# Graph attention kernel: value products joined two pairs at a time, softmax norms spread in two parts, last tile's messages pair by pair

## The reference, cut to what matters

```python
def _attention_message(Q, K, V, senders, receivers, n_nodes):
    scores = jnp.einsum('ehd,ehd->eh', Q[receivers], K[senders]) * scale
    smax = jax.ops.segment_max(scores, receivers, num_segments=n_nodes)
    ex = jnp.exp(scores - smax[receivers])
    denom = jax.ops.segment_sum(ex, receivers, num_segments=n_nodes)
    att = ex / denom[receivers]
    out = jax.ops.segment_sum(att[:, :, None] * V[senders], receivers, num_segments=n_nodes)
    return (out, att)
...
out = msg.reshape(n_nodes, HEADS * DV) @ W_ff.T + b_ff
```

## Time and profile before

| | |
|---|---|
| median of three runs | 321.08 us (320.94 to 321.26) |
| the profiled execution | 321.26 us, its span 319.5 us |
| TensorE busy, weight loads | 294.4 us (92% of the span), 226.4 us |
| VectorE, ScalarE, GpSimd busy | 194.0, 142.9, 69.8 us |
| chain that ended last | TensorE 81%, VectorE 12%, ScalarE 3%, issue 2% |
| TensorE's granted clock | full in all 40 slices |
| attention stage | from 219 us to the end |

### The profile page before, as it was taken

The page is one execution under the profiler, slowest core; times in us unless marked ns, Lnnn a source line. Parts: engine busy times, 40 slices in busy tenths (PEclk is TensorE's granted clock), DMA queues, the critical chain, the costliest instruction groups (busy, mean ns, idle before and its releaser), DMA issues.

```text
span 319.5 us, 5460 instructions
## 1 busy us (share of the span) xinstructions
PE 294.4 (92%) x2006; PEld 226.4 (71%) x2006; DVE 194.0 (61%) x471; ACT 142.9 (45%) x282; POOL 69.8 (22%) x97
## 2 busy tenths in 40 slices
PE   2848699999999999998999999997999999999994
PEld 1513345544677788687887889997888898888882
DVE  5899977986234344334359744967857565565721
ACT  1152234523325322533343505687876464665621
POOL 6045003210655044800012402310002020020202
PEclk9999999999999999999999999999999999999999
DMA  5753992111080300045300000000000000000000
GB/s 181 251 209 131 331 386 106 67 36 55 17 291 8 133 2 2 2 131 139 125 0 0 2 0 3 0 3 0 2 0 2 36 0 35 1 2 35 1 35 29
DMA packets 10970, 22.29 MB, mean 70 GB/s; under 512 B 950, under 2 KB 966, under 8 KB 10938
## 3 DMA queue, kind: packets, MB, share of 16 engines
q1 hardware_dynamic: 8772, 16.80, 15.3%
q0 software_dynamic: 800, 2.62, 2.2%
q10 hardware_dynamic: 1366, 2.45, 2.1%
HBM read 15.60 MB, written 6.26 MB: 68 GB/s over the span
## 4 chain that ended last, share of the span: by engine, by line
PE 81%; DVE 12%; ACT 3%; issue 2%; DMA 1%; DVEq 0%; POOL 0%
PE banks L1239 15%; PE banks L1185 9%; PE banks L1225 9%; PE banks L1325 8%; PE banks L1130 8%; PE banks L1311 7%; PE banks L1300 7%; PE banks L1083 5%; PE banks L1345 5%; DVE key_hot L820 3%; DVE row_hot L827 2%; PE banks L1215 2%; PE banks L1335 2%; PE banks L1172 1%; PE banks L1202 1%
## 5 line engine op out<-in xcount | busy, mean ns | idle before, releaser
L1003 DVE CUSTOM_DVE_ANT_0 s_sb<-banks,mask_add 128x640 f32<-128x640 f32 x40 | 32.6, 822 | 22.2 <-PE banks L1300 22.1
L1083 PE MATMUL banks<-key_hot,row_hot 128*128 128x480 f16 x120 | 32.5, 419 | 9.0 <-DVE key_hot L820 9.0
L660 ACT ACTIVATE p_sb<-s_sb,neg_max 128x640 f32<-128x640 f32 x40 | 32.9, 823 | 17.3 <-DVE neg_max L1003 17.3
L820 DVE TENSOR_SCALAR key_hot<-iota,picked 128x480 f16<-128x480 f16 x120 | 36.9, 374 | 0.0
L1185 PE MATMUL banks<-adjT,h 128*128 128x320 f16 x240 | 33.1, 299 | 0.4 <-DVE zT_even L879 0.4
L1083 PEld LDWEIGHTS banks<-key_hot,row_hot 128*128 128x128 f16 x120 | 12.6, 105 | 26.4 <-DVE key_hot L820 9.2
L1185 PEld LDWEIGHTS banks<-adjT,h 128*128 128x128 f16 x240 | 23.3, 98 | 9.8 <-DVE zT_even L879 0.7
L1311 PE MATMUL banks<-ident,p_sb 128*128 128x128 f32 x200 | 29.6, 275 | 0.2 <-ACT pT L667 0.2
L490 POOL TENSOR_TENSOR msgT<-msg_f,msgT 128x128 fp32r<-128x128 f32 x20 | 8.6, 458 | 95.7 <-ACT msgT L681 95.7
L1239 PE MATMUL banks<-w_hl,zT_even 128*128 128x512 f32 x120 | 29.2, 394 | 0.0
L1300 PE MATMUL banks<-k_hi,q_st 128*128 128x320 f32 x80 | 27.1, 348 | 2.0 <-DVE neg_max L1003 2.0
(11 more groups left out here) (176 smaller groups left out, 466.4 us busy)
## 6 DMA issues: line engine op xcount, KB each, us to landing
w_self<-in_L_gnn_W_self_dram SPq DMA_DIRECT2D x3, 1024.0 KB, 9.4
raw<-in_L_gnn_W_rel_dram SPq DMA_DIRECT2D x3, 1024.0 KB, 15.6
raw<-in_L_gnn_W_qkv_dram SPq DMA_DIRECT2D x3, 1024.0 KB, 5.3
sorted_rows<-zero_rows ACTq DMA_DIRECT2D x1, 1792.0 KB, 10.7
self_rows<-hs SPq DMA_DIRECT2D x7, 256.0 KB, 2.0
hs<-sorted_rows SPq DMA_DIRECT2D x1, 1280.0 KB, 7.2
xs<-in_x_dram SPq DMA_DIRECT2D x1, 1024.0 KB
raw<-in_L_gnn_W_ff_dram SPq DMA_DIRECT2D x1, 1024.0 KB
```

The lines of the kernel that those rows point to most:

```text
L660: nc.scalar.activation(p_sb[:, n % NPR, :], s_sb[:, n % NS, :], ACT.Exp, scale=-1.0, bias=neg_max[:, it, h:h + 1], accum_out=denom[:, it, ...
L820: return nc.vector.tensor_scalar(to_key, iota[:], float(KEYS * w), key, ALU.add, ALU.is_equal)
L1003: nc.vector.tensor_tensor_reduce(s_sb[:, n % NS, :].rearrange("p (a j) -> p a j", a=2), banks[:, c:c + 2, 0:HALF], mask_add[:, it, :].rear ...
L1083: mm(banks[:, w % 2, 0:KEYS], row_hot[:, w % 2, k, :], key_hot[:, w % 2, k, :], start=(k == 0), stop=True, skip_group_check=True).then_inc ...
```

## The change

Five parts:

1. **pv by twos.** The first pair of each two is placed at the second's place, so two pairs' products stand together, 40 instructions in the trace, at ten places instead of nineteen.
2. **norms in two parts.** VectorE spreads the eight norms to 128x512 itself (a broadcast copy into a float32r high part, then a subtraction for the low part), and rb becomes eight float32r products of 128 held columns with `ident_r` (128 columns) over all PSUM partitions. `norm` has one buffer instead of two, so norm n waits for rb n-1.
3. **`ident_r`**, a float32r copy of `ident`, is made on GpSimd at the start. `bounds` and `bounds_f` move to another place in SBUF.
4. **Banks of the last tile.** Its four pairs write banks 0 to 3 (the scores' banks, free after the last smax) instead of quarters of bank 4.
5. **Messages of the last tile.** Each waits for its own pair's pv alone.

```diff
-        placed += [(at, "pv", n) for n, at in enumerate(pv_at)]
+        placed += [(pv_at[n // 2 * 2 + 1], "pv", n) for n in range(NT * KD)]
...
+                pair_at = [max(pv_at[it * KD + a // 2 * 2 + 1], it * H + RB) + 0.1 for a in range(KD)]
+                placed += [(pair_at[a], "msg", it * KD + a) for a in range(KD)]
+                placed += [(pair_at[-1] + FF_STEP * kt, "ff", it * KD + kt) for kt in range(KD)]
+                placed.append((pair_at[-1] + FF_STEP * KD, "out", it))
...
+        def pv_place(it, a):
+
+            return banks[:, 4, a * P:(a + 1) * P] if it < NT - 1 else banks[:, a, 0:P]
...
+            nc.gpsimd.tensor_copy(ident_r[:], ident[:]).then_inc(s_ident, 1)
...
                 elif kind == "norm":
                     dve.wait_ge(s_exp, H * (n + 1))
-                    if n >= 2:
-                        dve.wait_ge(s_rb, n - 1)
+                    if n >= 1:
+                        dve.wait_ge(s_rb, n)
                     chain(nc.vector.reciprocal(recip[:, n % 2, :], denom[:, n, :]))
-                    nc.vector.scalar_tensor_tensor(out=norm[:, n % 2, :], in0=neg_max[:, n, :], scalar=BIG / 2,
-                                                   in1=recip[:, n % 2, :], op0=ALU.is_lt, op1=ALU.mult
-                                                   ).then_inc(s_norm, 1)
+                    chain(nc.vector.scalar_tensor_tensor(out=norm[:], in0=neg_max[:, n, :], scalar=BIG / 2,
+                                                         in1=recip[:, n % 2, :], op0=ALU.is_lt, op1=ALU.mult))
+                    spread = norm[:].unsqueeze(2).broadcast_to([P, H, DK])
+                    chain(nc.vector.tensor_copy(norm_hl[:, 0], spread))
+                    nc.vector.tensor_tensor(norm_hl[:, 1], spread, norm_hl[:, 0].bitcast(F32),
+                                            ALU.subtract).then_inc(s_norm, 1)
                 elif kind == "msg":
                     it, a = divmod(n, KD)
+                    if it == NT - 1:
+                        dve.wait_ge(s_pv, n + 1)
+                    elif a == 0:
+                        dve.wait_ge(s_pv, KD * (it + 1))
                     if a == 0:
-                        dve.wait_ge(s_pv, KD * (it + 1))
                         dve.wait_ge(s_rsb, it + 1)
...
-                    if a == 0 and it >= 1:
+                    if a == 0 and it == NT - 1:
+                        pe.wait_ge(s_smax, NT * H)
+                    elif a == 0 and it >= 1:
                         pe.wait_ge(s_msg, KD * it)
...
-                    for h in range(H):
-                        me = 64 * (h % 2)
-                        ins = mm(banks[me:me + 64, 7, h // 2 * P:(h // 2 + 1) * P],
-                                 norm[:, n % 2, h:h + 1].broadcast_to([P, DK]), ident[:],
-                                 start=(h < 2), stop=True, skip_group_check=True)
+                    for a in range(KD):
+                        for p in range(2):
+                            ins = mm(banks[:, 7, a * P:(a + 1) * P],
+                                     norm_hl[:, p, 2 * a:2 * a + 2, :].rearrange("p h d -> p (h d)"),
+                                     ident_r[:], start=(a == 0 and p == 0), stop=(p == 1), skip_group_check=True)
```

More of the change, by code:

```diff
@@ L81, in gnn_kernel @@
         ident = sb("ident", [P, P], F32)
+        ident_r = sb("ident_r", [P, P], F32R)
         ident16 = sb("ident16", [P, P], F16)
@@ L106, in gnn_kernel @@
         place_u = sb("place_u", [P, NT], U32)
-        bounds = sb("bounds", [1, 3, 32], I32)
-        bounds_f = sb("bounds_f", [1, 4, 32], F32)
         stats = sb("stats", [P, NT, 6], F32)
@@ L118, in gnn_kernel @@
         recip = sb("recip", [P, 2, H], F32)
-        norm = sb("norm", [P, 2, H], F32)
+        norm = sb("norm", [P, H], F32)
         Z_BYTES = 2 * KD * NP * 4
@@ L160, in gnn_kernel @@
         ones = place("ones", o_r4 + 60768, [P, P], F32)
+        bounds = place("bounds", o_r4 + 64000, [1, 3, 32], I32)
+        bounds_f = place("bounds_f", o_r4 + 64384, [1, 4, 32], F32)
         tile_iota = place("tile_iota", o_r4 + 61280, [P, 8], F32)
@@ L186, in gnn_kernel @@
         self_d = nc.dram_tensor("self_rows", [SP, D], F32, kind="Internal").ap()
+        norm_hl = place("norm_hl", o_r4 + 35328, [P, 2, H, DK], F32R)
         banks = ctx.enter_context(nc.psum_tensor("banks", [P, 8, 512], F32))
         s_fill = sem("s_fill")
+        s_ident = sem("s_ident")
         s_edges = sem("s_edges")
@@ L325, in gnn_kernel @@
             placed += [((it + 1) * H, "norm", it), (it * H + RB, "rb", it)]
-            placed += [(msg_at, "msg", it * KD + a) for a in range(KD)]
-            placed += [(msg_at + FF + FF_STEP * kt, "ff", it * KD + kt) for kt in range(KD)]
-            placed.append((msg_at + FF + FF_STEP * (KD - 1) + 0.1, "out", it))
+            if it < NT - 1:
+                placed += [(msg_at, "msg", it * KD + a) for a in range(KD)]
+                placed += [(msg_at + FF + FF_STEP * kt, "ff", it * KD + kt) for kt in range(KD)]
+                placed.append((msg_at + FF + FF_STEP * (KD - 1) + 0.1, "out", it))
+            else:
+                pair_at = [max(pv_at[it * KD + a // 2 * 2 + 1], it * H + RB) + 0.1 for a in range(KD)]
+                placed += [(pair_at[a], "msg", it * KD + a) for a in range(KD)]
+                placed += [(pair_at[-1] + FF_STEP * kt, "ff", it * KD + kt) for kt in range(KD)]
+                placed.append((pair_at[-1] + FF_STEP * KD, "out", it))
         attention = [(kind, n) for _, kind, n in sorted(placed, key=lambda step: step[0])]
@@ L1031, in _ @@
                         dve.wait_ge(s_mlo, n + 1 - KD)
-                    nc.vector.tensor_tensor(msg_f[:, a], banks[:, 4, a * P:(a + 1) * P], r_sb[:, a],
+                    nc.vector.tensor_tensor(msg_f[:, a], pv_place(it, a), r_sb[:, a],
                                             ALU.mult).then_inc(s_msg, 1)
@@ L1324, in _ @@
                             h = 2 * a + hh
-                            ins = mm(banks[64 * hh:64 * hh + 64, 4, a * P:(a + 1) * P],
+                            ins = mm(pv_place(it, a)[64 * hh:64 * hh + 64],
                                      v_sb[:, jt, h * DK:(h + 1) * DK], pT[:, s, :],
@@ L1332, in _ @@
                         pe.wait_ge(s_fin, n)
-                    for h in range(H):
-                        me = 64 * (h % 2)
-                        ins = mm(banks[me:me + 64, 7, h // 2 * P:(h // 2 + 1) * P],
-                                 norm[:, n % 2, h:h + 1].broadcast_to([P, DK]), ident[:],
-                                 start=(h < 2), stop=True, skip_group_check=True)
+                    if n == 0:
+                        pe.wait_ge(s_ident, 1)
+                    for a in range(KD):
[3 more added lines that the diff above has]
+                                     ident_r[:], start=(a == 0 and p == 0), stop=(p == 1), skip_group_check=True)
                     ins.then_inc(s_rb, 1)
```

## The result

The changed kernel takes 316.15 us (median of four, 315.79 to 316.51) against 321.16 beside it: a ratio of 0.9839, 95% interval 0.9825 to 0.9853. Forecast were 315.6, in a range from 314.7 to 318.0. A second set of runs of the same kernel gave 315.93 against 321.45, a ratio of 0.9828 (0.9813 to 0.9843). The profiled execution took 315.79, its span is 314.0 where it was 319.5.

What follows compares the result with a forecast made beforehand. TensorE's row of work was taken to bound the kernel. Savings of 1.08 + 2.64 + 0.5 + 1.29 = 5.5 us, counted from the median of 321.08, gave 315.6, in a range from 314.7 to 318.0.

Steps and rivals of the forecast that it cites:

- What bounds: Attention stage: nearly every piece is TensorE's, one behind the other; a tile's period falls from 18.74 to 17.7 to 17.8 us.
- Value products and exits: TensorE's value products: ten joined rows save 1.08 us, fewer exits from the 64-column form save 2.64.
- rb: TensorE's rb: eight full-width float32r products at 0.115 us each take 0.92 instead of 1.02, saving 0.5 over five.
- The rule that I weighed: At rb: weight loads overlap products only in different row groups, so eight cost 1.32 us and the total is 317.6.
- End of the last tile: Behind the last value products: TensorE runs the last ffs without waiting for messages, 4.27 to 2.98 us, saving 1.29.
- VectorE's new work at nothing: Cast and subtraction at tile ends, 1.3 us per tile, hidden with 0.9 to spare at the first tile, 3.6 later.
- The rival on the slower side: VectorE bounds each tile's end: new operations before an awaited smax are exposed five times, 6.8 us, giving 322.4; chance 0.04.
- Longer stretches at nothing: Between value products: four scores and five turns run without TensorE waiting, though ScalarE falls behind 0.06 us a head; cost nothing.

Runs made afterwards that it cites:

- join_only: The kernel before with only the joining of value products by twos, old rb, bank and messages kept; 318.24 us against 321.37, ratio 0.9902.
- split: The changed kernel with other work, mostly a turn and a score, between the pairs of nine of ten twos; 318.58 us, ratio 0.9915 to the kernel before.
- tail_only: The kernel before with only the last tile's banks and pair-by-pair messages of the change, nothing joined; 319.91 us, ratio 0.9948.
- norm_x3: The changed kernel with VectorE's spreading cast and subtraction made four times in each norm; 325.82 us, ratio 1.0147 to the kernel before.
- norm_x1: The changed kernel with VectorE's spreading cast and subtraction made twice in each norm; 316.58 us, ratio 0.9858 to the kernel before.

## Why the prediction was right, point by point

- *What bounds.* Right: TensorE's row of work is the time, 1.01 less per tile (forecast 17.7 to 17.8 for the period, measured 17.73).
- *Value products and exits* (1.08 + 2.64). Right in mechanism and nearly in size: 40 take 2.33 (forecast 2.345), the last 40 included, so ten rows take 23.3 and the first term was 1.23; the turn behind them 0.59 (0.58). `join_only`, forecast 2.7, gave 2.87 in the stage, and `split`, forecast 2.6, gave 2.64, with two things left out of the forecast that cancel. Reading the same instructions at different lengths in one chain was enough to price a cost that has no row of its own.
- *rb* (0.92, from bounds of 0.44 and 1.75). Measured 0.84, 0.105 a product, so the choice near the turn's 0.11 was right and 0.4 too dear over five. Against it the score behind rb keeps 0.06 of its old 0.20, four times, which I had at nothing: 0.24. The rule that I weighed (a weight load overlaps running products only in other rows, rb then 1.32) doesn't hold here: load and columns together took 0.105, not 0.165. The Trainium skill, page "TensorE: Matmul & The Clock Gate", section "LDWEIGHTS (loading the stationary operand)", gives a load as its columns divided by 1.2, by which I estimate 107 ns for 128. The 0.84 to 0.89 for eight agree with loads that alone set the pace; no run here changed the load and left the rest, so this is not shown.
- *End of the last tile* (1.29). Measured 4.27 - 2.96 = 1.31, in `tail_only` 1.30.
- *VectorE's new work at nothing.* Right as to the result, 0.43 + 0.69 a tile and hidden (the cast cheaper than the 0.59 of its nearest row, so VectorE is busy 5.1 more and not 6 to 7). The working behind it was wrong: 3.6 to spare in later tiles, and 0.9 in the first, counted when TensorE wants one smax and not the fills and exps that come after it on both engines. `norm_x3` showed it, with every period 1.25 longer where it should have lost nothing or 0.5, and `norm_x1`, where 1.2 more cost 0.6 at the first tile. The rival on the slower side was much nearer than I put it.
- *Longer stretches at nothing.* This is the step that failed, by a small amount. I took a stretch of four scores and five turns without a wait as proof. That was misread: from 225.34 to 229.09 there are three scores and four turns, and the score and the turn ahead of them, which make up the four and five, are parted from them by a wait for a fill. The timeline of the kernel before:

```profile
225.34 0.63 PE L1311 MATMUL banks<-ident,p_sb 128*128 128x128 f32 x4 [0.18 <-ACT pT L667]
```

And in the first tile that very stretch grows by two scores and two turns, because the pair that ended it has moved. TensorE waits there for a fill and loses 0.36. The engine was not the one that I had priced, either: I had ScalarE fall behind by 0.06 a head, and the fill was VectorE's. In later tiles nothing waits.

Sum, of what the pieces measured: 1.23 + 2.64 + 0.9 - 0.24 + 1.31 - 0.36 = 5.5, and the stage lost 5.43. The forecast was 5.5 as well, and that it fits so well is partly luck: value products and rb gave 0.15 + 0.4 more than forecast, and the score behind rb and the wait in the first tile, both at nothing in the forecast, took back 0.24 + 0.36.

## What to carry to other kernels

When TensorE's chain has no gaps, look for the same instructions at different lengths, and at what stands before them: products in half the array between products in the whole cost 0.33 a visit here, and moving visits together costs nothing as long as the other engines' buffers carry the longer stretch. To say how much work an engine can take on, follow everything that starts later because of it, in its queue and in the queues of the engines that it feeds, until the next wait that matters, and not only the one instruction behind the new work. And before a part is split into high and low, ask whether the gain is the data type's or the shape's.

## What the runs showed that I had not expected

Eight products that hold and move 128 columns over the whole array take 0.84 in float32r, and the eight instructions of four float32 products take 0.89. One float32r product costs half a float32 one, but splitting in two parts needs twice as many, so at this shape the split gains nothing. And the price of a visit to the 64-column form lies only at its ends: 40 value products take 2.33 and 80 take 4.52, 0.055 for each of the further ones. Last, a late smax costs TensorE nothing where its next score comes late enough, and costs it two turns of 0.63 all the same, a few steps later, by way of ScalarE's exps and fills (`norm_x1`).
